# A graph network on one core: squares of the second edge layer summed on VectorE, scatters in chunks of their own

## The chip, the cores and the metric

The kernel runs on one core of one Trainium2 chip. The metric is device time in microseconds of one execution, from which the median of several runs is taken; smaller is better. The engines are PE (TensorE: matrix products, with its weight loads shown apart as PEld), DVE (VectorE), ACT (ScalarE), POOL (GpSimd) and SP (SyncE, here only a queue of DMA issues).

## The reference

Four graph layers follow one another on 12,500 nodes of 32 features and 400,000 edges that are sorted by their destination, each with a residual and a layer norm behind it. The change lies in the second of them and reaches back into the first. Cut to that:

```python
x = _layernorm(x + agg0)                      # layer 0: agg0[dst] += (x * out_norm)[src], times in_norm
row, col = edge_index                         # src, dst
h = concatenate([x[row], edge_attr_32], 1)    # 400000 x 64
h = lrelu(bn(h, g1, b1) @ w1 + c1)            # first edge layer,  64 -> 64
h = lrelu(bn(h, g2, b2) @ w2 + c2)            # second edge layer, 64 -> 64, slope 0.1
h = bn(h, g3, b3) @ w3 + c3                   # needs mean and mean square of h over the edges
agg = segment_sum(h, col)                     # 12500 x 64
h2 = concatenate([x, agg], 1)                 # node layers: three more products with bn before each
...
x = _layernorm(x + out)
```

The third layer (attention) wants the edges sorted by their source. For it the kernel builds a bucket sort: each edge's pair (src, dst) is written to a computed place of a table in HBM.

## The kernel before

**Tiling.** 400,000 edges are 625 groups of 640 edges: 128 partitions by T = 5. A loop turn takes SLOTS = 5 groups (ITERS = 125 turns), and each of its five slots has its own buffers. Every stage is a block in which each engine runs its own hand-written program; semaphores tie them together, and all engines meet between stages.

**Sums over destinations.** Nodes lie in 98 blocks of 128. A group touches one block, or a few. `one_hot` (line 107) compares the group's destination keys with a ramp 0..127, less the block's start, on DVE; it takes two tensors, `keys` and `ramp`, and a column of `starts` as scalar. PE multiplies the one-hot by the group's rows into PSUM bank 7 (line 162), and DVE adds the bank to the accumulator `acc` (line 138). There are 722 such visits for 625 groups: 97 times the group crosses into a further block, and then PE waits for a second one-hot. Layer 0 (`stage_convolve`) and the second edge layer (`stage_edges_second`) use these helpers. In layer 0, POOL gathers the rows by indirect DMA, five of 128 rows for each group (line 547).

**The second edge layer**, for each group: SP loads the activations `a1` of the first edge layer from HBM and the group's `pair` (lines 823, 826). PE multiplies them by the folded weights into bank 0 or 1 (line 898). DVE adds the bias row (`lift2`, line 874), makes the one-hot (line 107), and takes max(lift, 0.1 lift) into `rows` (line 879). ACT squares the rows (line 844), and PE sums the squares over the edges with products of 64 by 1 (line 906). Then comes the visit (lines 162 and 138). PE and DVE run one group ahead with the first half and one behind with the second (`in_turn`).

**The scatters.** Beside this, POOL issues for every group five indirect DMAs that write 128 pairs each to the bucket table (line 921), 3,125 in all. Their places come from `places`, which the first edge layer computed as floats; ACT turns a group's five columns into integers (`place`, line 838), in program order between two squares, and waits there until the slot's former scatters have landed:

```python
for j in range(SLOTS):
    square(i, j)
    act.wait_ge(s["moved"][j], 16 * T * (i + 1))
    place(i + 1, j)
```

**The node layers** (`stage_nodes`) follow: sums, transposes slab by slab, three products over 25 chunks of 500 nodes, and a layer norm. POOL has no program in this stage. After it `stage_source_keys` reads the bucket table.

## Time and profile before

| what | value |
|---|---|
| time, median of 3 runs | 29849.66 us (29847.4 to 29855.73) |
| profiled execution, its own time (first to last instruction) | 29897.7 us |
| PE busy over the whole | 24784.2 us (83%) |
| DVE busy | 17947.6 us (60%) |
| POOL busy | 16752.9 us (56%) |
| ACT busy | 4472.9 us (15%) |
| layer 0, first to last gather | 903.9 to 4884.5 us |
| second edge layer, first to last scatter | 9108.2 to 13208.2 us |
| node layers | 13220 to 13725 us |

All times inside the profile count from the span's start. "Busy" sums the instructions of an engine; "idle before" is what the engine stood still ahead of a group of instructions, with what ended it. On POOL, "issue" is the time between one indirect DMA and the next in which it waited for nothing that the profile shows.

### The profile page before, as it was taken

How to read it: one execution, taken by the hardware profiler on the slowest of the kernel's cores; microseconds unless marked ns; L12 is line 12 of the kernel's file. 1: busy time of each engine (PE TensorE's matmuls, PEld its weight loads, DVE VectorE, ACT ScalarE, POOL GpSimd, SP SyncE). 2: the span in 40 equal slices, each digit the busy share in tenths (PEclk: the TensorE clock that was granted, in tenths of full speed). 3: DMA queues.
4: the chain of work that ended last, by engine and by line, in shares of the span. 5: the costliest groups of instructions: out<-in, count | busy, mean ns of one | idle time of the engine just before them, and what ended most of it. 6: DMA issues, size and time to landing. Idle time of an engine off the chain costs nothing. (4 is left out here: it accounts for less than half of the span.)

```text
span 29897.7 us, 608296 instructions
## 1 busy us (share of the span) xinstructions
PE 24784.2 (83%) x149627; PEld 16178.0 (54%) x149628; DVE 17947.6 (60%) x47075; ACT 4472.9 (15%) x12240; POOL 16752.9 (56%) x16857
## 2 busy tenths in 40 slices
PE   8777776666668999986999998665888898898988
PEld 6444443222227888863666776664444444444444
DVE  9311114666664333333666665887777777778777
ACT  4111111111110000001111111221111111111111
POOL 0677776777777777752777776453333333333332
PEclk9555555555555555555666555997999999999999
DMA  2111112222221111103333336553333333333332
GB/s 66 36 30 30 30 30 44 51 50 50 51 50 28 27 27 27 27 17 41 80 79 80 79 78 64 164 172 107 74 75 74 74 73 74 74 75 75 73 75 68
DMA packets 2615646, 1869.05 MB, mean 63 GB/s; under 512 B 1600555, under 2 KB 2081065, under 8 KB 2613814
## 3 DMA queue, kind: packets, MB, share of 16 engines
q1 hardware_dynamic: 1914438, 1424.41, 19.2%
q0 software_dynamic: 516000, 217.22, 7.1%
q10 hardware_dynamic: 184400, 220.54, 2.9%
q14 instruction: 776, 6.36, 0.1%
q8 instruction: 32, 0.52, 0.0%
HBM read 1621.01 MB, written 238.82 MB: 62 GB/s over the span
## 5 line engine op out<-in xcount | busy, mean ns | idle before, releaser
L2069 POOL DMA_INDIRECT rows_x<-x_table,index x3125 | 3044.3, 974 | 6251.2 <-DMA index<-in_src 5485.0
L1310 POOL DMA_INDIRECT rows<-x_table,index x3625 | 3446.2, 951 | 2029.3 <-issue 1255.0
L162 PE MATMUL banks<-rows,onehot 128*128 128x33 f32 (+1 forms) x14440 | 3416.9, 413 | 1065.9 <-issue 592.0
L547 POOL DMA_INDIRECT rows<-x_table,index x3125 | 3029.3, 969 | 1853.6 <-issue 928.2
L162 PEld LDWEIGHTS banks<-rows,onehot 128*128 128x128 f32 x14440 | 3186.1, 328 | 1374.0 <-issue 1364.7
L921 POOL DMA_INDIRECT bucket_pairs<-pair,place_int x3125 | 3148.4, 1007 | 1012.2 <-issue 952.5
L696 POOL DMA_INDIRECT rows<-x_table,index x3125 | 3143.5, 1006 | 1019.6 <-issue 952.0
L1929 PE MATMUL banks<-first,same_unit 128*128 128x384 f32 (+1 forms) x10000 | 3504.7, 476 | 0.0
L1220 DVE CUSTOM_DVE_ANT_0 junk<-banks,mask 128x320 f32<-128x320 f32 x5800 | 2551.6, 487 | 1560.6 <-PE banks L1255 1538.5
L1778 DVE TENSOR_TENSOR second<-banks,h 128x384 f32<-128x384 f32 (+1 forms) x5000 | 2276.1, 485 | 690.5 <-PE banks L1929 681.1
L1770 DVE TENSOR_TENSOR first<-banks,h 128x768 f32<-128x768 f32 x2500 | 2054.9, 822 | 836.7 <-issue 442.5
L138 DVE TENSOR_TENSOR acc<-acc,banks 128x33 f32 (+1 forms) x1444 | 298.4, 207 | 3388.3 <-PE banks L162 3388.3
L1929 PEld LDWEIGHTS banks<-first,same_unit 128*128 128x128 f32 x10000 | 1824.2, 203 | 895.5 <-issue 511.3
L1917 PE MATMUL banks<-u_turned,w_tensor 32*128 32x384 f32 (+1 forms) x10000 | 2096.2, 496 | 250.1 <-DVE first L1770 235.3
L1255 PE MATMUL banks<-x_turned,vectors_wide 32*128 32x320 f32 x11600 | 2163.4, 718 | 0.0
L107 DVE SCALAR_TENSOR_TENSOR onehot<-keys,starts,ramp 128x640 f32<-128x640 f32 x1444 | 1279.1, 886 | 1344.5 <-issue 1344.5
L790 PE MATMUL banks<-ident,rows 128*64 128x128 f32 x3125 | 777.7, 415 | 1276.2 <-DMA rows<-x_table,index 1276.2
L1244 PE MATMUL banks<-ident,rows 128*32 128x128 f32 x29000 | 1542.0, 388 | 316.3 <-DMA rows<-x_table,index 314.1
L1244 PEld LDWEIGHTS banks<-ident,rows 128*32 128x32 f32 x29000 | 1189.4, 156 | 904.3 <-issue 846.5
L1267 PEld LDWEIGHTS banks<-vectors_four,x_turned 32*128 32x128 f32 x7250 | 1405.3, 282 | 346.8 <-issue 346.8
L1917 PEld LDWEIGHTS banks<-u_turned,w_tensor 32*128 32x128 f32 x10000 | 779.1, 190 | 1413.6 <-DVE first L1770 790.6
L1427 PE MATMUL banks<-rows,onehot 128*128 128x132 f32 x7250 | 1099.8, 304 | 520.9 <-POOL rows L1363 517.0
(396 smaller groups left out, 38909.6 us busy)
## 6 DMA issues: line engine op xcount, KB each, us to landing
key_row<-key_rows SPq DMA_DIRECT2D x1450, 320.0 KB
h<-hidden_dram SPq DMA_DIRECT2D x10000, 40.0 KB
key_row<-dst_rows SPq DMA_DIRECT2D x625, 320.0 KB
rows<-x_table,index POOLq DMA_INDIRECT x9875
a_dram<-a ACTq DMA_DIRECT2D x625, 160.0 KB
a<-a_dram SPq DMA_DIRECT2D x625, 160.0 KB
rows_dram<-rows ACTq DMA_DIRECT2D x725, 90.0 KB
x_rows<-rows_dram SPq DMA_DIRECT2D x725, 90.0 KB
```

What stands on the lines that cost most here:

```text
L162: mm = nc.tensor.matmul(m["ps"][7][:, 0:width], m["onehot"][j % 3][:, t * P:(t + 1) * P], rows[:, t, :], start=t == 0, stop=t == T - 1)
L547: nc.gpsimd.indirect_dma_start(out=m["rows"][j][:, t * W:t * W + F], out_offset=None, in_=m["x_table"], in_offset=bass.IndirectOffsetOnAxi ...
L696: nc.gpsimd.indirect_dma_start(out=m["rows"][j][:, t * C2:t * C2 + F], out_offset=None, in_=m["x_table"], in_offset=bass.IndirectOffsetOnA ...
L921: nc.gpsimd.indirect_dma_start(out=m["bucket_pairs"], out_offset=bass.IndirectOffsetOnAxis(ap=m["place_int"][j][:, t:t + 1], axis=0), in_= ...
L1220: nc.vector.tensor_tensor_reduce(m["junk"][j % 3][:, HALF * u:HALF * (u + 1)], bank(j, u), m["mask"][j % 3][:, HALF * half:HALF * (half + 1)],
L1244: mm = nc.tensor.matmul(m["ps"][6 + t // 4][F * h:F * (h + 1), t % 4 * P:(t % 4 + 1) * P], m["rows"][j][:, t * XA:t * XA + F], m["ident"][ ...
L1255: nc.tensor.matmul(bank(j, half * HEADS + h), m["vectors_wide"][rows, h * P:(h + 1) * P], m["x_turned"][j][rows, half * HALF:(half + 1) * ...
L1310: nc.gpsimd.indirect_dma_start(out=m["rows"][j][:, t * XA:t * XA + F], out_offset=None, in_=m["x_table"], in_offset=bass.IndirectOffsetOnA ...
L1778: nc.vector.tensor_tensor(m["second"][2 * (q % 2) + k][:, columns(half)], m["ps"][6 + k][:, 0:HALVES[half][1]], m["h2"][j][:, columns(half ...
L1917: mm = nc.tensor.matmul(m["ps"][4 + k][:, 0:HALVES[half][1]], m["w_tensor"][rows, chunk * P:(chunk + 1) * P], m["u_turned"][j % 3][rows, c ...
L1929: nc.tensor.matmul(m["ps"][6 + k][:, 0:width], m["same_unit"][:, :], m["first"][q][:, k * width:(k + 1) * width], start=True, stop=True).t ...
L2069: nc.gpsimd.indirect_dma_start(out=m["rows_x"][j][:, t * F:(t + 1) * F], out_offset=None, in_=m["x_table"], in_offset=bass.IndirectOffsetO ...
```

## The change

- The sum of squares leaves PE: ACT writes the squares into PSUM bank 5, and DVE adds them to `square_acc`, 128 by 320, for each group. After the loop PE sums that once, with five products.
- The bias becomes a 65th row of the weights, against a row of ones in `a1`. DVE's pass of line 874 goes. ACT makes 0.1 times the product (`lift2`), and DVE takes the maximum of the product in PSUM and `lift2`.
- The ramp is copied into PSUM bank 4, and `one_hot` reads it there, in layer 0 too.
- The places are written as integers in the first edge layer, and ACT's conversion goes. Pairs and places are loaded by SP in chunks of 25 columns, five chunks in flight, with no tie to the groups; ACT's queue issues the loads of `a1`.
- The scatters split: 22 turns of 125 (2,750) in the second edge layer, and 3 turns (375) in the node layers.
- PE's next product into a bank now waits for `a2_made`, the maximum, where it waited for `lifted`.

```diff
+RAMP_BANK = 4
 def one_hot(nc, m, g, j, at):
     return nc.vector.scalar_tensor_tensor(cut(m["onehot"][j % 3][:, :], t=T), rep(m["keys"][:, bass.ds(T * g, T)], 2, P),
-                                          m["starts"][:, bass.ds(at, 1)], rep(m["ramp"][:, :], 1, T),
+                                          m["starts"][:, bass.ds(at, 1)], rep(m["ps"][RAMP_BANK][:, 0:P], 1, T),
                                           ALU.subtract, ALU.is_equal)
...
             link(nc.vector.memset(m["acc"][:, 0:NB * W], 0.0))
+            link(nc.vector.tensor_copy(m["ps"][RAMP_BANK][:, 0:P], m["ramp"][:, :]))
...
-    nc.vector.tensor_reduce(m["places"][:, bass.ds(g * T, T)], cut(m["picked"][:, :], t=T), AX.X, ALU.add).then_inc(s["placed"], 1)
+    with nc.allow_low_precision(reason="one term of each sum is a whole number below 2 ** 24, the others are zero"):
+        nc.vector.tensor_reduce(m["places"][:, bass.ds(g * T, T)], cut(m["picked"][:, :], t=T), AX.X, ALU.add).then_inc(s["placed"], 1)
...
+SCATTER_FIRST = 22
+SCATTER_LAST = ITERS // SLOTS - SCATTER_FIRST
+def scatter_loads_sp(sp, m, s, first, turns):
+
+    width = SLOTS * T
+
+    def load(i, k):
+        at = ((first + i) * SLOTS + k) * width
+        sp.dma_start(m["pair"][k][:, :], m["pairs"][:, bass.ds(2 * at, 2 * width)]).then_inc(s["pair_in"][k], 16)
+        sp.dma_start(m["place_int"][k][:, :], m["places"][:, bass.ds(at, width)]).then_inc(s["pair_in"][k], 16)
+    for k in range(SLOTS):
+        load(0, k)
+    with sp.Fori(1, turns) as i:
+        for k in range(SLOTS):
+            sp.wait_ge(s["moved"][k], 16 * width * i)
+            load(i, k)
+
+
+def scatter_pool(nc, pool, m, s, turns):
+
+    width = SLOTS * T
+    with pool.Fori(0, turns) as i:
+        for k in range(SLOTS):
+            pool.wait_ge(s["pair_in"][k], 32 * (i + 1))
+            pool.sem_inc(s["going"], 1)
+            for c in range(width):
+                nc.gpsimd.indirect_dma_start(
+                    out=m["bucket_pairs"], out_offset=bass.IndirectOffsetOnAxis(ap=m["place_int"][k][:, c:c + 1], axis=0),
+                    in_=m["pair"][k][:, 2 * c:2 * c + 2], in_offset=None,
+                ).then_inc(s["moved"][k], 16)
+    for k in range(SLOTS):
+        pool.wait_ge(s["moved"][k], 16 * width * turns)
+
+
...
             sp.dma_start(m["sb_m1_c2"][:, :], m["m1_c2"].broadcast_to([P, H])).then_inc(s["weights"], 16)
-
-            def load(i, j, again):
-                g = SLOTS * i + j
-                sp.wait_ge(s["products"][j], ONE + i)
-                sp.dma_start(m["a1"][j][:, :], m["a1_dram"][bass.ds(g, 1)].rearrange("g h e -> (g h) e")).then_inc(s["a1_in"][j], 16)
-                if again:
-                    sp.wait_ge(s["moved"][j], 16 * T * i)
-                sp.dma_start(m["pair"][j][:, :], m["pairs"][:, bass.ds(g * 2 * T, 2 * T)]).then_inc(s["pair_in"][j], 16)
-            for j in range(SLOTS):
-                load(0, j, False)
-            with sp.Fori(1, ITERS) as i:
-                for j in range(SLOTS):
-                    load(i, j, True)
+            scatter_loads_sp(sp, m, s, 0, SCATTER_FIRST)
...
-            def place(i, j):
-                nc.scalar.copy(m["place_int"][j][:, :], m["places"][:, bass.ds((SLOTS * i + j) * T, T)]).then_inc(s["placed"][j], 1)
-
-            def square(i, j):
+            def load(i, j):
+                act.dma_start(m["a1"][j][0:H, :], m["a1_dram"][bass.ds(SLOTS * i + j, 1)].rearrange("g h e -> (g h) e")
+                              ).then_inc(s["a1_in"][j], 16)
+
+            def lift(i, j):
                 g = SLOTS * i + j
+                act.wait_ge(s["products"][j], ONE + i + 1)
+                act.wait_ge(s["a2_made"], ONE + g)
+                nc.scalar.activation(m["lift2"][:, :], m["ps"][j % 2][:, 0:T * H], ACT.Copy, scale=SLOPE).then_inc(s["lifted"], 1)
+
+            def square(i, j, again):
+                g = SLOTS * i + j
+                if again:
+                    load(i + 1, j)
                 act.wait_ge(s["a2_made"], ONE + g + 1)
                 act.wait_ge(s["squares_used"], ONE + g)
-                nc.scalar.square(cut(m["squares"][:, :], t=T), cut(m["rows"][j][:, 0:T * W], t=T)[:, :, 0:H]).then_inc(s["squared"], 1)
+                nc.scalar.square(cut(m["ps"][5][:, 0:T * H], t=T), cut(m["rows"][j][:, 0:T * W], t=T)[:, :, 0:H]).then_inc(s["squared"], 1)
+            act.wait_ge(s["unit_rows"], ONE + 1)
             for j in range(SLOTS):
-                place(0, j)
+                load(0, j)
+            lift(0, 0)
             with act.Fori(0, ITERS - 1) as i:
                 for j in range(SLOTS):
-                    square(i, j)
-
-                    act.wait_ge(s["moved"][j], 16 * T * (i + 1))
-                    place(i + 1, j)
+                    lift(i + (j + 1) // SLOTS, (j + 1) % SLOTS)
+                    square(i, j, True)
             for j in range(SLOTS):
-                square(ITERS - 1, j)
+                if j < SLOTS - 1:
+                    lift(ITERS - 1, j + 1)
+                square(ITERS - 1, j, False)
...
             link(nc.vector.memset(m["acc"][:, 0:NB * W], 0.0))
+            link(nc.vector.tensor_copy(m["ps"][RAMP_BANK][:, 0:P], m["ramp"][:, :]))
+            link(nc.vector.memset(m["square_acc"][:, :], 0.0))
+            for j in range(SLOTS):
+                link(nc.vector.memset(m["a1"][j][H:H + 1, :], 1.0))
+            nc.vector.nop().then_inc(s["unit_rows"], 1)
...
-            link(nc.vector.tensor_tensor(m["bias_row"][:, :], m["sb_m1_c2"][:, :], m["ps"][0][:, 0:H], ALU.add))
...
             def ahead(i, j):
                 g = SLOTS * i + j
-                dve.wait_ge(s["products"][j], ONE + i + 1)
-                dve.wait_ge(s["a2_made"], ONE + g)
-                nc.vector.tensor_tensor(cut(m["lift2"][:, :], t=T), cut(m["ps"][j % 2][:, 0:T * H], t=T),
-                                        rep(m["bias_row"][:, :], 1, T), ALU.add).then_inc(s["lifted"], 1)
                 hot_dve(nc, dve, m, s, g, j)
                 dve.wait_ge(s["lifted"], ONE + g + 1)
-                lift = cut(m["lift2"][:, :], t=T)
-                nc.vector.scalar_tensor_tensor(cut(m["rows"][j][:, 0:T * W], t=T)[:, :, 0:H], lift, SLOPE, lift,
-                                               ALU.mult, ALU.max).then_inc(s["a2_made"], 1)
-            in_turn(dve, ahead, lambda i, j: visits_dve(nc, dve, m, s, SLOTS * i + j, j, m["acc"], W))
+                nc.vector.tensor_tensor(cut(m["rows"][j][:, 0:T * W], t=T)[:, :, 0:H], cut(m["ps"][j % 2][:, 0:T * H], t=T),
+                                        cut(m["lift2"][:, :], t=T), ALU.max).then_inc(s["a2_made"], 1)
+
+            def behind(i, j):
+                g = SLOTS * i + j
+                visits_dve(nc, dve, m, s, g, j, m["acc"], W)
+                dve.wait_ge(s["squared"], ONE + g + 1)
+                dve.wait_ge(s["squares_used"], ONE + g)
+                nc.vector.tensor_tensor(m["square_acc"][:, :], m["square_acc"][:, :], m["ps"][5][:, 0:T * H], ALU.add
+                                        ).then_inc(s["squares_used"], 1)
+            in_turn(dve, ahead, behind)
             sums_done(nc, dve, m, s)
-            dve.wait_ge(s["squares_used"], ONE + GROUPS)
+            dve.wait_ge(s["square_totals"], ONE + 1)
             nc.vector.tensor_copy(m["square_sum"][0:H, :], m["ps"][2][0:H, 0:1])
...
-            nc.tensor.matmul(m["ps"][2][0:H, 0:1], m["zeros"][:, 0:H], m["zero_row"][:, 0:1], start=True, stop=False, skip_group_check=True)
...
             def ahead(i, j):
                 pe.wait_ge(s["a1_in"][j], 16 * (i + 1))
-                pe.wait_ge(s["lifted"], ONE + (SLOTS * i + max(j - 1, 0)))
+                pe.wait_ge(s["a2_made"], ONE + (SLOTS * i + max(j - 1, 0)))
                 for t in range(T):
-                    mm = nc.tensor.matmul(m["ps"][j % 2][:, t * H:(t + 1) * H], m["a1"][j][:, t * P:(t + 1) * P],
-                                          m["w"][0:H, 0:H], start=True, stop=True)
+                    mm = nc.tensor.matmul(m["ps"][j % 2][:, t * H:(t + 1) * H], m["a1"][j][0:W, t * P:(t + 1) * P],
+                                          m["w"][0:W, 0:H], start=True, stop=True)
                 mm.then_inc(s["products"][j], 1)
             def behind(i, j):
                 g = SLOTS * i + j
-                pe.wait_ge(s["squared"], ONE + g + 1)
-                for t in range(T):
-                    mm = nc.tensor.matmul(m["ps"][2][0:H, 0:1], m["squares"][:, t * H:(t + 1) * H], m["ones"][:, 0:1],
-                                          start=False, stop=False, skip_group_check=True)
-                mm.then_inc(s["squares_used"], 1)
                 pe.wait_ge(s["a2_made"], ONE + g + 1)
                 visits_pe(nc, pe, m, s, g, j, cut(m["rows"][j][:, 0:T * W], t=T), W)
             in_turn(pe, ahead, behind)
+            pe.wait_ge(s["squares_used"], ONE + GROUPS)
+            for t in range(T):
+                mm = nc.tensor.matmul(m["ps"][2][0:H, 0:1], m["square_acc"][:, t * H:(t + 1) * H], m["ones"][:, 0:1],
+                                      start=t == 0, stop=t == T - 1)
+            mm.then_inc(s["square_totals"], 1)
         @block.gpsimd
         def _(pool):
-            with pool.Fori(0, ITERS) as i:
-                for j in range(SLOTS):
-                    pool.wait_ge(s["placed"][j], ONE + i + 1)
-                    pool.wait_ge(s["pair_in"][j], 16 * (i + 1))
-                    pool.sem_inc(s["going"], 1)
-                    for t in range(T):
-                        nc.gpsimd.indirect_dma_start(
-                            out=m["bucket_pairs"], out_offset=bass.IndirectOffsetOnAxis(ap=m["place_int"][j][:, t:t + 1], axis=0),
-                            in_=m["pair"][j][:, 2 * t:2 * t + 2], in_offset=None,
-                        ).then_inc(s["moved"][j], 16)
-            for j in range(SLOTS):
-                pool.wait_ge(s["moved"][j], 16 * T * ITERS)
+            scatter_pool(nc, pool, m, s, SCATTER_FIRST)
...
             sp.wait_ge(s["cleared"], ONE + 1)
             sp.dma_start(m["c3_row"][H:H + 1, :], m["m1_c3"]).then_inc(s["weights"], 16)
+            scatter_loads_sp(sp, m, s, SCATTER_FIRST, SCATTER_LAST)
+
+        @block.gpsimd
+        def _(pool):
+            scatter_pool(nc, pool, m, s, SCATTER_LAST)
...
         sb("acc", NB * (H + 1), into=whole)
+        sb("places", COLS, I32, into=whole)
+        for name, cols in (("pair", 2 * SLOTS * T), ("place_int", SLOTS * T)):
+            m[name] = [whole.enter_context(nc.sbuf_tensor(f"{name}{k}", [P, cols], I32)) for k in range(SLOTS)]
```

## Rows read from the trace of the kernel before

**Rows 1.** Window of the second edge layer: us, busy of PE, PEld, DVE, ACT, POOL, granted clock.
```profile
9109.00:13209.00 4100.00, 3867.08 (x19722) 3682.89 (x19721) 1360.06 (x2695) 394.62 (x1245) 3147.46 (x3125) 0.50 0.13 26
```

**Rows 2.** Groups of the second edge layer: busy us, mean ns, idle before.
```profile
L921 POOL DMA_INDIRECT bucket_pairs<-pair,place_int x3125 | 3148.4, 1007 | 1012.2 <-issue 952.5 <-ACT place_int L838 59.7
L162 PE MATMUL banks<-rows,onehot 128*128 128x65 f32 x7220 | 1727.8, 423 | 171.9 <-DVE onehot L107 171.9
L898 PE MATMUL banks<-w,a 64*128 64x64 f32 x6250 | 1494.9, 423 | 0.2 <-DVEq L868 0.2
L906 PE MATMUL banks<-ones,squares 128*64 128x1 f32 x6250 | 765.4, 247 | 59.7 <-ACT squares L844 59.7
L107 DVE SCALAR_TENSOR_TENSOR onehot<-keys,starts,ramp 128x640 f32<-128x640 f32 x722 | 639.9, 886 | 407.5 <-issue 407.5
L874 DVE TENSOR_TENSOR lift<-banks,bias_row 128x320 f32<-128x320 f32 x625 | 307.4, 492 | 1224.2 <-PE banks L898 1224.1
L879 DVE SCALAR_TENSOR_TENSOR rows<-lift 128x320 f32<-128x320 f32 x625 | 302.7, 484 | 0.0
L844 ACT ACTIVATE squares<-rows 128x320 f32<-128x320 f32 x625 | 293.5, 470 | 61.0 <-DVE rows L879 32.5 <-issue 25.2
L138 DVE TENSOR_TENSOR acc<-acc,banks 128x65 f32 x722 | 161.2, 223 | 1107.4 <-PE banks L162 1107.4
```

**Rows 3.** Line 921, all scatters: ns min/median/max, first and last start.
```profile
L921 POOL DMA_INDIRECT bucket_pairs<-pair,place_int x3125: 954/958/1609, 9108.2 to 13208.2; - x196
```

**Rows 4.** Timeline of one turn: start, duration, engine, line, and what released it.
```profile
11002.12 2.39 PE L898 MATMUL banks<-w,a 64*128 64x64 f32 x10
...
11004.45 1.23 PE L906 MATMUL banks<-ones,squares 128*64 128x1 f32 x10
11004.55 0.49 DVE L874 TENSOR_TENSOR lift<-banks,bias_row 128x320 f32<-128x320 f32 x1 [1.98 <-PE banks L898]
11004.58 0.96 POOL L921 DMA_INDIRECT bucket_pairs<-pair,place_int  x1 [0.30 <-issue]
...
11005.60 2.39 PE L162 MATMUL banks<-rows,onehot 128*128 128x65 f32 x10
11005.70 0.89 DVE L107 SCALAR_TENSOR_TENSOR onehot<-keys,starts,ramp 128x640 f32<-128x640 f32 x1 [0.65 <-issue]
11005.85 1.57 POOL L921 DMA_INDIRECT bucket_pairs<-pair,place_int  x1 [0.30 <-issue]
...
11007.92 2.39 PE L898 MATMUL banks<-w,a 64*128 64x64 f32 x10
```

**Rows 5.** First and last of the 196 long scatters in 9500 to 11500.
```profile
9508.28 1.28 POOL L921 DMA_INDIRECT bucket_pairs<-pair,place_int  x1 [0.30 <-issue]
...
11495.42 1.20 POOL L921 DMA_INDIRECT bucket_pairs<-pair,place_int  x1 [0.30 <-issue]
```

**Rows 6.** Line 547, the gathers of the first stage of sums: ns min/median/max, idle.
```profile
L547 POOL DMA_INDIRECT rows<-x_table,index x3125: 940/944/1605, 903.9 to 4884.5; - x196
...
  issue: 928.2, 3045
```

**Rows 7.** Timeline at the start and the end of the second edge layer.
```profile
9100.49 0.59 SPq L826 DMA_DIRECT2D pair<-in_pairs  x1
...
9109.54 4.52 PE L898 MATMUL banks<-w,a 64*128 64x64 f32 x20 [0.23 <-DVEq L868]
...
13219.94 0.50 SPq L944 DMA_DIRECT2D sb_m_w<-in_m_w  x1
```

**Rows 8.** Timeline of the node layers: last load, last VectorE work, next stage.
```profile
13229.75 0.28 SPq L946 DMA_DIRECT2D c_row<-in_m_c  x1
...
13713.36 3.43 DVE L91 TENSOR_TENSOR tmp<-x 128x3136 f32<-128x3136 f32 x1
...
13726.56 0.40 SPq L315 DMA_DIRECT2D block_dram<-block_int  x1
```

**Rows 9.** Group of the node layers' bend, over 13209.5 to 13726.
```profile
L1030 DVE SCALAR_TENSOR_TENSOR h<-node_lift 96x500 f32 x50 | 33.7, 675 | 128.2 <-ACT node_lift L965 128.2
```

15 lines of the change are left out of this document (7 added, 8 removed).

## The prediction

> **What bounds the kernel now.** I read the page first: over the whole, PE is the busiest engine, but that is a mean over eight stages. The change touches three of them (layer 0, the second edge layer, the node layers), so each is read by itself. In the second edge layer the window shows PE 3867 of 4100 us busy and POOL 3147, at a granted clock of 0.50, TensorE's lower level of 1.2 GHz [rows 1]. Busy time misleads here, because issue time does not count. The groups show it: the 3,125 scatters are busy 3148.4 us and have 952.5 us of issue ahead of them [rows 2], together 4100.9 us. That is the whole way from the first scatter at 9108.2 to the end of the last at about 13209.1 [rows 3]. POOL never waits for another engine after its start. It is the bound, at 4100.9 / 3,125 = 1.312 us a scatter.
>
> PE is close behind. One group without a second visit takes 11007.92 - 11002.12 = 5.80 us on PE: 2.32 for line 898, 1.16 for line 906, 2.32 for line 162 [rows 4]. The 97 further visits cost 171.9 / 97 = 1.77 us of waiting for the one-hot and 2.32 us of product each. 625 x 5.80 + 97 x 4.09 + 59.7 of waiting for squares [rows 2] = 3625 + 397 + 60 = 4082 us, against 4098 from 9109.5 to 13207.8. So the wait for squares is all the slack PE has: ACT's conversion of places, in program order between the squares, holds PE to POOL's pace. Taking 725 us off PE alone would bring at most that little; the scatters must go too.
>
> **Scatters that take longer.** The scatter has a median of 958 ns and a mean of 1007, with a maximum of 1609 [rows 2, 3]: 3,125 x 0.049 = 153 us are lost to long ones. In the turn shown, the long scatter starts at 11005.85, inside the one-hot of 11005.70 to 11006.59, and ends 0.83 us after that one-hot; the scatter at 11004.58 runs beside line 874 and takes its 0.96 us [rows 4]. Between 9500 and 11500, 196 of 1,524 scatters are over 1.01 us [rows 5], and 194 of them started while a one-hot was running (two beside line 879 alone, whose input lies twice in SBUF); of 256 that started beside line 138 or 874, with one operand in PSUM, none was long. The gathers of layer 0 show the same: median 944 ns, maximum 1605 [rows 6]. My reading: a DVE instruction with two tensors in SBUF keeps POOL from reading its indices.
>
> The Trainium skill, "SBUF — State Buffer", section "Who interferes with whom", says as much: a DVE instruction with two SBUF inputs contends with a GpSimd instruction that reads SBUF, one with at most one does not. By that rule all long scatters vanish with the ramp in PSUM, and the sum comes out as below.
>
> **Part by part. Scatters in the second edge layer.** 2,750 remain. The pitch without long ones is 0.958 + 952.5 / 3,124 = 1.263 us, so 2,750 x 1.263 = 3473 us. The kept DVE work has one operand in PSUM in every instruction of the loop (one-hot, maximum, addition to `acc`, addition of squares). The unknown is whether the one-hot, which still has `keys` and the scalar column in SBUF, lets POOL through. Bounds: fully, as beside lines 138 and 874, 3473; not at all, 2,750 x 1.312 = 3609, 136 more. I take the first, since those rows are the nearest in kind. Below it, the least duration of 954 ns [rows 3] would give another 11. Waiting every 25 scatters in place of every 5 I cost at nothing: the issue time before the scatters is the same 0.30 whether a group begins or not. The first scatter no longer waits for ACT's conversion: SP's queue reached its first pair at 9100.49 [rows 7]; with its place load behind it (0.59 to issue) and some 2 us to land it starts between 9102 and 9108; I take 9104. End: 9104 + 3473 = 12577, against 13209: **-632 us**.
>
> **PE must keep ahead of that.** Line 906 goes (1.16 us a group); line 898 has 65 rows for 64, at no cost, as line 162 with 128 rows has the same mean of 423 ns [rows 2]. 625 x 4.64 + 397 = 3297 us. It starts later than 9109.5 [rows 7] by DVE's new preparation (a copy, six fills); seven times the 0.89 of the 640 elements of line 107 is the most, nothing the least; I take 4. End: 9113.5 + 3297 = 12411, 166 us ahead of POOL, or 0.27 us a group. This slack covers the new waits. For the slot that wraps (j = 0), PE needs the maximum of the group just multiplied: 2.43 us from line 898's start to its reader's [rows 4], 0.49 for the lift on ACT (470 ns for a square of this size), 0.49 for the maximum (492 for line 874), some 0.3 of handing over: 3.7, while PE has 2.32 + 2.32 = 4.64 us of other work. DVE does, in each group, 722 / 625 x (0.886 + 0.564 issue + 0.223) + 2 x 0.49 = 2.9 us; ACT two passes of 0.47 to 0.49 and one issue of at most 0.59, about 1.6. Both lie inside 4.64. If the cover were gone, each us a group would cost 625. The `a1` loads, moved from SP's queue to ACT's, are issued more than three groups (14 us) before their use; SP's queue, which now waits for landed scatters, has only scatter loads behind that wait.
>
> The ramp in PSUM may slow the one-hot. Line 874, with a PSUM operand, takes 492 ns, line 879, with none, 484 [rows 2]: 8 ns for 320 elements, so some 10 to 16 ns, in work that DVE does inside PE's 4.64 us.
>
> The Trainium skill, "VectorE: DVE Perf Modes", section "The TRN2 errata", gives 120 fixed cycles for a PSUM source and 58 for an SBUF source, an estimate of 65 ns more a one-hot. These rows do not show it (8 ns); by the page the further visits would cost PE 97 x 0.065 = 6 us, inside the slack as well.
>
> **Layer 0.** From the first gather to the last, 4884.5 - 903.9 = 3980.6 us for 3,124 pitches; at 0.944 + 928.2 / 3,045 = 1.249 us [rows 6] they take 3901. **-79 us** if the one-hot lets POOL through, 0 if not. POOL is the bound: the issue rows and its durations fill the stage.
>
> **Node layers.** The 375 scatters start behind SP's last weight load at 13229.75 (times of before) [rows 8]: two issues of 0.59 and some 2 us give 13233. 375 x 1.263 = 474, to 13707. The bend of line 1030 has both tensors in SBUF, 50 times 0.675 us [rows 9]. A start falls inside one with a chance of 0.675 / 1.263 and loses 0.34: 9 us, 13716. Then the layer norm's passes of 3.43 us, such as 13713.36 [rows 8], can hold back what is left: three of them have two SBUF tensors, 10 us at most, with the landing 13728, while before the next stage starts at 13726.56. Between 0 and 15; I take **+2**. DVE's own delay by POOL is within this: the one-hot's maximum in such company stayed under 1 us.
>
> **Sum.** -632 - 79 + 2 = -709. The profiled execution has a span of 29897.7, 48 us (0.16%) above the median of the runs; it would come to 29189, and the median to 29849.7 - 709 = **29141 us**, 2.4% faster.
>
> **Rivals.**
> 1. *The one-hot still blocks POOL*, by `keys` or by the scalar column. For it: I have no row with one SBUF tensor, a scalar column and a PSUM tensor. Against: lines 138 and 874 block nothing. Price: 136 + 79 = 215, so 29356.
> 2. *The node layers do not hide the scatters*: the many small chained DVE steps and POOL hold each other up, or the scatters start late. For it: POOL ends within 10 us of the stage. All 375 uncovered would add 474; I price a quarter, 120: 29261.
> 3. *The PE loop becomes the bound*, because bank, ACT and DVE form a chain in each group: 2.43 + 0.49 + 0.49 + 0.3 + 2.32 = 6.03 us. Then the loop takes 625 x 6.03 + 397 = 4166, ends at 13280, 71 later than before, and with layer 0 the time is 29844: no change. It shows from 4.90 us a group on. Against: the order of `in_turn` puts a product of the other group under the chain.
> 4. *Slower*: the same chain also takes in the square on ACT and its addition on DVE, because each waits for the other through the single `lift2` and bank 5: 6.03 + 0.47 + 0.49 + 0.2 = 7.2 us a group. 625 x 7.2 + 397 = 4897, end 14011, +802 - 79 + 2: 30575. It decides from 6.04 us a group. Against it speaks that the sum of squares comes behind the visit in DVE's order, a whole PE product after its input.
>
> **How the numbers follow.** Forecast 0.75, rival 1 0.10, rival 2 0.07, rival 3 0.05 (of which 0.03 lands within 0.2%), rival 4 0.03. The forecast's own range is 29113 (least durations, earliest start) to 29170 (preparation at its most, 15 us in the node layers, some long scatters left). With rivals 1 and 2 the range is 29112 to 29360. A difference under 0.2% (60 us) is about what a measurement of this kernel cannot tell from none. Faster 0.94, same 0.03, slower 0.03.
>
> **What would show it.** Scatters of line 921 with a maximum near 970 ns in the second edge layer, and a stage 632 us shorter; gathers of layer 0 near 0.944 each and the stage 79 us shorter; PE's group at 4.64 us, with idle time it did not have; node layers of about 505 us with 375 scatters in them. I am wrong if scatters over 1.1 us remain beside the one-hots, if PE's groups take 4.9 us or more, or if the stage after the node layers starts more than 15 us late.

## The result and the profile after

The changed kernel takes 29103.83 us (median of 4 runs, 29053.54 to 29111.04) beside 29848.53 us for the kernel before (4 runs): ratio 0.9746, 95% interval 0.9734 to 0.9758, 745 us faster. The forecast was 29141 us with a range from 29112: the direction and nearly the whole size are as forecast, but the time lies 37 us below the forecast and 8 us below the range. The profiled execution of the changed kernel took 29098.85 us (a span of 29096.7 from first to last instruction), that of the kernel before has a span of 29897.7.

Groups of the second edge layer in the changed kernel (9020 to 12517 us), beside [rows 2]:
```profile
L840 POOL DMA_INDIRECT bucket_pairs<-pair,place_int x2750 | 2641.9, 961 | 892.3 <-issue 837.2 <-DMA place_int<-places 55.0
L165 PE MATMUL banks<-rows,onehot 128*128 128x65 f32 x7220 | 1695.4, 418 | 172.6 <-DVE onehot L110 172.1 <-DVE acc L141 0.5
...
L945 PE MATMUL banks<-w,a 65*128 65x64 f32 x6250 | 1460.3, 421 | 0.7 <-DVEq L913 0.7
...
L110 DVE SCALAR_TENSOR_TENSOR onehot<-keys,starts,banks 128x640 f32<-128x640 f32 x722 | 635.4, 880 | 478.3 <-issue 478.3
L919 DVE TENSOR_TENSOR rows<-banks,lift 128x320 f32<-128x320 f32 x625 | 305.5, 489 | 22.2 <-ACT lift L874 14.7
L927 DVE TENSOR_TENSOR square_acc<-square_acc,banks 128x320 f32<-128x320 f32 x625 | 304.7, 488 | 153.3 <-issue 146.4
L882 ACT ACTIVATE banks<-rows 128x320 f32<-128x320 f32 x625 | 275.9, 442 | 193.4 <-issue 190.8 <-DVE square_acc L927 2.6
L874 ACT ACTIVATE lift<-banks 128x320 f32<-128x320 f32 x625 | 273.6, 438 | 2330.9 <-PE banks L945 2330.9
L141 DVE TENSOR_TENSOR acc<-acc,banks 128x65 f32 x722 | 160.7, 223 | 1043.1 <-PE banks L165 1043.1
```
The mean scatter has gone from 1007 to 961 ns, and the group of squares has left TensorE. POOL still never waits for an engine once it runs. ACT's lift (line 874, 0.1 times the product) and square take 0.44 us each in the mean, and the maximum of line 919 waits 14.7 us in all for the lifts.

The windows of 1000 us in the middle of the stage, of the kernel before and of the changed one (us, then busy us and count of PE, PEld, DVE, ACT, POOL, granted clock, DMA share, GB/s):
```profile
10000.00:11000.00 1000.00, 942.69 (x4811) 897.76 (x4812) 332.96 (x659) 96.13 (x304) 767.64 (x763) 0.50 0.13 27
```
```profile
10000.00:11000.00 1000.00, 943.32 (x4385) 937.44 (x4385) 448.42 (x878) 178.87 (x408) 759.40 (x791) 0.50 0.16 35
```
POOL issues 791 scatters where it issued 763. The granted clock is 0.50 in both, the lower level of 1.2 GHz, so the clock gives nothing here.

One turn of the changed kernel, beside [rows 4]:
```profile
11000.72 2.34 PE L945 MATMUL banks<-w,a 65*128 65x64 f32 x10
...
11002.75 0.88 DVE L110 SCALAR_TENSOR_TENSOR onehot<-keys,starts,banks 128x640 f32<-128x640 f32 x1 [0.65 <-issue]
11002.85 2.34 PE L165 MATMUL banks<-rows,onehot 128*128 128x65 f32 x10
11002.92 0.96 POOL L840 DMA_INDIRECT bucket_pairs<-pair,place_int  x1 [0.30 <-issue]
...
11004.99 1.27 PE L945 MATMUL banks<-w,a 65*128 65x64 f32 x5
```
The scatter at 11002.92 starts inside the one-hot and takes 0.96 us, where its like in [rows 4] took 1.57. PE's group is 11004.99 - 11000.72 = 4.27 us; the prediction had 4.64.

All scatters of the changed kernel, those beside the node layers included, and the gathers of layer 0 (ns min/median/max, first and last start), beside [rows 3, 6]:
```profile
L840 POOL DMA_INDIRECT bucket_pairs<-pair,place_int x3125: 955/962/4077, 9026.6 to 13007.7; - x196
```
```profile
L551 POOL DMA_INDIRECT rows<-x_table,index x3125: 941/947/1092, 902.8 to 4810.8; - x196
```

Of the 2,750 scatters in the second edge layer none is over 1.01 us (before: 407 of 3,125). The 13 that are lie beside the node layers: 12 start inside the bend (line 1030 before, 1071 here), which reads two SBUF tensors, and the one of 4077 ns is shown below.

Start and end of the second edge layer and of the node layers, beside [rows 7, 8]:
```profile
9020.40 0.50 SPq L858 DMA_DIRECT2D sb_m_w<-in_m_w  x1
...
9026.57 1.00 POOL L840 DMA_INDIRECT bucket_pairs<-pair,place_int  x1 [55.04 <-DMA place_int<-places]
...
12110.55 1.23 PE L956 MATMUL banks<-ones,square_acc 128*64 128x1 f32 x10 [1.22 <-DVE square_acc L927]
...
12504.71 0.96 POOL L840 DMA_INDIRECT bucket_pairs<-pair,place_int  x1 [0.30 <-issue]
12517.71 0.51 SPq L980 DMA_DIRECT2D sb_m_w<-in_m_w  x1
...
12530.52 0.96 POOL L840 DMA_INDIRECT bucket_pairs<-pair,place_int  x1 [24.85 <-DMA place_int<-places]
...
13007.54 3.42 DVE L90 TENSOR_TENSOR x<-x,mean 128x3136 f32<-128x3136 f32 x1
13007.72 4.08 POOL L840 DMA_INDIRECT bucket_pairs<-pair,place_int  x1 [0.31 <-issue]
...
13024.27 0.40 SPq L318 DMA_DIRECT2D block_dram<-block_int  x1
```
From SP's first DMA of one stage to that of the next, the second edge layer takes 12517.71 - 9020.40 = 3497.3 us (before 4122.4), the node layers 13024.27 - 12517.71 = 506.6 us, exactly as before (13726.56 - 13219.94 [rows 7, 8]), with 375 scatters in them. The last of these meets a layer-norm step with two SBUF tensors: it takes 4.08 us and ends 0.84 us after that step, the same tail as that of the long scatters before; there was room for it.

Where the time came from (us, from the first profiles of the two kernels; the attention gather and the tensor product are counted from their first gather to their last, and the attention sum is what lies between them):

| | before | after | forecast | measured |
|---|---|---|---|---|
| layer 0, first to last gather | 3980.6 | 3908.0 | -79 | -72.6 |
| second edge layer | 4122.4 | 3497.3 | -632 | -625.1 |
| node layers | 506.6 | 506.6 | +2 | 0.0 |
| start of the source keys' stage | 13726.6 | 13024.3 | -709 | -702.3 |
| attention gather | 4763.2 | 4748.0 | 0 | -15 |
| attention sum | 2113.5 | 2070.3 | 0 | -43.2 |
| tensor product | 9001.4 | 8962.6 | 0 | -39 |

Not all of these repeat. Two more profiles of the kernel before and one more of the changed program (before_again, before_b and pad_pe below) have 4744 to 4763 us in the attention gather against 4748 to 4752, so no difference; 8978 to 9014 in the tensor product against 8960 to 8963; 2109 to 2115 in the attention sum against 2068 to 2070; and in layer 0 3977 to 3981 against 3900 to 3908.

### The profile page after: what moved, and what is told of

It is laid out like the page before. It is cut to its first block and busy times, and to the rows that moved or that the text cites. A ratio compares the mean times of both kernels' runs of the same rounds, so it can differ in the third digit from the quotient of the medians.

```text
span 29096.7 us, 592714 instructions
## 1 busy us (share of the span) xinstructions
PE 23725.4 (82%) x143386; PEld 15329.1 (53%) x143387; DVE 17957.4 (62%) x47083; ACT 4626.8 (16%) x12240; POOL 16532.3 (57%) x16857
## 5 line engine op out<-in xcount | busy, mean ns | idle before, releaser
L840 POOL DMA_INDIRECT bucket_pairs<-pair,place_int x3125 | 3009.3, 963 | 1031.0 <-issue 951.1
L110 DVE SCALAR_TENSOR_TENSOR onehot<-keys,starts,banks 128x640 f32<-128x640 f32 x1444 | 1270.8, 880 | 1398.0 <-issue 1398.0
```

Source lines behind the costliest of these rows:

```text
L840: nc.gpsimd.indirect_dma_start(out=m["bucket_pairs"], out_offset=bass.IndirectOffsetOnAxis(ap=m["place_int"][k][:, c:c + 1], axis=0), in_= ...
```

## The experiments

Two conditions of the machine were met, and the reader needs them for the numbers. The comparison above and two more sessions (one with before_again, the ramp kernels and no_split, one with before_b, compute_only and pad_pe) found the kernel before at 29,849 to 29,900 us; I call this the undisturbed condition. Three others found it at 35,788, 36,242 and 35,802 us, every run of them alike; the first of these was on the chip that in a later session gave 29,856. I call that the other condition. Whole times are compared only within a session, as ratios or differences to the kernel before of that session; durations of stages are compared across sessions of one condition.

**The kernel before once more** (before_again, before_b; no edit).

> The kernel before, unchanged, for its stages. From the start of the stage behind the node layers to the end it took 16171 us in the first profile, and the changed kernel took 16072 there with the same code. Theory A (executions differ by chance in these stages): this profile shows 16110 to 16150 there, and the time is within 0.1% of before. Theory B (the change shortens the later stages too): it shows 16171 again, within 10 us.

> The kernel before, for its trace. If the chip is one of the slower kind (some 36,000 us): theory, that GpSimd's unbroken stream of scatters holds back the semaphores of TensorE, expects its second edge layer near 5,100 us (35,788 us less the other stages of the changed kernel's trace there), thus 1,500 us less than the changed kernel's 6,625, with groups that wait on other engines less than the changed kernel's 56 us a group. Rival: that chip's loads are slow for both; then TensorE waits for its load of a1 (landing well over the 13 us after issue seen in the changed kernel on both kinds of chip). If the chip is of the first kind: 29,850 to 29,900 us, the second edge layer 4,122 us, the attention sum 2,113 us.

Measured: 29881.27 us, ratio 1.0 (0.9991 to 1.001), and 29868.42 us, ratio 1.0004 (0.9994 to 1.0014). So two sets of ten and more runs of one kernel agree within 0.1%; with four runs the interval is some 0.17% either way. The second edge layer took 4122.0 and 4122.9 us, the attention sum 2114.5 and 2108.7, within 6 us of the first profile. From the start of the source keys' stage to the end it is 16145 and 16158 us where the first profile has 16171. The 16145 lies in the interval of theory A: a part of what the first pair of profiles shows in these stages is chance. The changed program has 16072 and 16073 (pad_pe) there, so 72 to 99 us of difference are left, which repeats alone do not explain.

**The ramp alone** (ramp_only: before, with this) and **the ramp taken back** (ramp_back: after, without it).
```
-  ... rep(m["ramp"][:, :], 1, T), ...
+  ... rep(m["ps"][RAMP_BANK][:, 0:P], 1, T), ...
```


> The kernel before with the ramp in PSUM alone. Port theory (a one-hot with two SBUF tensors keeps POOL from starting a DMA): long scatters and gathers vanish, layer 0 is 73 us shorter. In the second edge layer POOL needs only 3,125 x 1.265 = 3953 us, PE needs 625 x 5.80 + 397 = 4022, so PE becomes the bound and the stage is 60 to 78 us shorter: 133 to 151 us in all. Rival (the ramp matters in layer 0 alone, since in the second layer the in-place maximum of line 879, twice from SBUF, blocks as well): 73 us in all.

> The changed kernel with the ramp read from SBUF again. Port theory: layer 0 is 73 us longer; in the second edge layer 722 one-hots at up to 0.21 us each stretch the scatters by 110 to 154 us, and POOL is the bound, so 183 to 227 us slower. Rival (the second layer's gain came from the other DVE edits): 73 us slower, with a mean scatter of 961 ns left.

Measured: 29739.12 us, ratio 0.9941 (0.9924 to 0.9957), 161 us faster than before (median 29900.49), with layer 0 at 3903.3 and the second edge layer at 4045.7 us. Taken back: 29344.65 us, 0.9812 (0.9796 to 0.9828); layer 0 3988.5, second edge layer 3645.3 us, that is 80.5 and 148 us more than in the changed kernel. The gathers of layer 0 with it taken back, then the scatters of the ramp alone:
```profile
L551 POOL DMA_INDIRECT rows<-x_table,index x3125: 940/945/1608, 903.4 to 4892.0; - x196
```
```profile
L926 POOL DMA_INDIRECT bucket_pairs<-pair,place_int x3125: 953/959/1285, 9033.6 to 13035.1; - x196
```
The maximum is back at 1608 in the one. In the other it falls to 1285: what is left are 182 scatters over 1.01 us, and all of them start inside line 884, which is this kernel's line 879 with its two SBUF operands; of the 424 that start inside a one-hot none is long. A one-hot with `keys` and the scalar column in SBUF but the ramp in the accumulator banks (PSUM) lets POOL through. Rival 1 did not come. The traces also say which starts are hit: in the kernel before, of the scatters that start in the first 0.1 us of a one-hot 0 of 167 are long, and of those that start between 0.1 and 0.7 us after its start all 395. Beside line 884 of ramp_only the edge lies earlier: all 35 that start 0.04 to 0.1 us into it are long. The Trainium skill, "SBUF — State Buffer", section "Who interferes with whom", has this rule of two SBUF inputs, and these runs agree with it.

**No scatters beside the node layers** (no_split).
```
-SCATTER_FIRST = 22
+SCATTER_FIRST = 25
```


> The changed kernel with all 3,125 scatters in the second edge layer and none beside the node layers. Theory (POOL is the bound of the second layer and the node layers hide theirs for nothing): 375 x 1.265 = 474 us slower, the node layers unchanged at 506.6 us. Rival (the 375 cost the node layers something, or PE bounds the second layer in part): clearly less, 430 us or under.

Measured: 29575.79 us, 0.9887 (0.9871 to 0.9904). The second edge layer took 3962.7 us, 465 more than after: 375 x 1.265 = 474 but for the landing. The node layers took 507.3 us without a scatter and 506.6 with 375. They hide all of them, so rival 2 did not come. This part is 465 us of the stage; of the whole time it is 420 us, by the differences to the kernel before in each session (325 us faster here, 745 for the changed kernel). The two medians themselves lie 472 us apart, but the kernel before also stood 52 us higher among the runs of no_split.

**The change without its scatter part** (compute_only: places converted on ACT, a pair tile a group, none beside the node layers; squares, bias row and ramp as changed).
```
 after's stage, with
+                    act.wait_ge(s["moved"][j], 16 * T * (i + 1))
+                    place(i + 1, j)
-            scatter_pool(nc, pool, m, s, SCATTER_FIRST)
+            with pool.Fori(0, ITERS) as i: ...   # as before
```


> The changed kernel with the scatters as in the kernel before (groups of five behind a conversion of the places on ScalarE, one pair tile a group, a1 from SyncE's queue, none beside the node layers); the squares, the bias row and the ramp stay changed. Chip of the first kind: GpSimd bounds the second edge layer at 625 x 6.35 to 6.47 = 3,970 to 4,045 us, the kernel 150 to 230 us faster than before plus 43 us of the attention sum: some 190 to 270 us faster. Chip of the slower kind: if the unbroken stream of scatters is what loses there, this kernel is faster than before (ratio 0.98 to 1.00) while the changed kernel stands at 1.05; if it is the squares or the bias edit, it stands near 1.05 too. The attention sum is near 2,070 to 2,080 us if the squares and bias edit is what shortens it, near 2,115 us if it is the scatter part.

Measured: 29575.25 us, 0.9903 (0.9886 to 0.9919), 281 us faster than before. Its scatters:
```profile
L941 POOL DMA_INDIRECT bucket_pairs<-pair,place_int x3125: 954/958/992, 9024.5 to 12968.1; - x196
```
3,125 at 1.262 us, no long one, stage 3970.9 us. In no_split, with chunks of 25, the way from the first scatter to the last is the same 3943.6 us: the size of the chunk costs nothing in POOL's pace. The 8 us between the two stages (3962.7 in no_split) lie ahead of the first scatter, which starts 15.4 and 6.0 us after SP's first DMA of the stage. So of the change's 625 us in this stage, about 150 are the long scatters, 465 the scatters that moved out, and some 8 the start. The squares and the bias edit have no share of their own: they keep TensorE out of the way of the rest. In ramp_only, which has neither, TensorE's products run from 9041.5 to 13064.0, 4022 us as the prediction counts them for its old loop, and end 28 us after the last scatter. There TensorE holds the stage, and only 77 of the 150 us come out.

**The changed kernel with empty instructions on TensorE** (pad_pe).

> The changed kernel with 190 empty instructions at the end of TensorE's program of the second edge layer, about as many as the change took out of it. Theory, that the attention sum and the tensor product run faster in the changed kernel because TensorE's later loops lie elsewhere in its program: the attention sum goes back from 2,070 to about 2,113 us and the tensor product's gathers by some 25 us, so 40 to 70 us slower than the changed kernel. Rival: the place in TensorE's program is nothing, and the cause lies elsewhere (the moment at which the clock and the loops meet, or the other engines' programs): attention sum 2,070 to 2,080 us. The 190 instructions themselves cost a few us at most.

The 190 empty instructions left none in the trace, so this was the changed kernel once more, and tells nothing on its theory: 29096.76 us, 0.9741 (0.9725 to 0.9758), 760 us faster than the kernel before of its session; layer 0 3899.7, second edge layer 3489.7, attention sum 2067.6 us. The result repeats.

**The product over 64 rows** (rows64, run in two sessions; the bias row is left out of the computation), and **the scatter part alone** (scatter_only, likewise; the squares on TensorE and the bias on DVE as before). Both ran in the other condition of the machine only, where the last part of the stage, after its last scatter, shows TensorE's loop by itself.
```
-  m["a1"][j][0:W, t * P:(t + 1) * P], m["w"][0:W, 0:H]
+  m["a1"][j][0:H, t * P:(t + 1) * P], m["w"][0:H, 0:H]
```


> The changed kernel with the product of the second edge layer over 64 rows, which leaves the bias row out of the computation. The prediction took TensorE's group at 4.64 us, from rows of a loop that goes to and fro between products of 64 rows and of 128; measured was 4.27 us with 65 rows. Theory: the change between a product of 64 rows and one of 128 costs time at each passage (starts 0.35 instead of 0.21 us apart), and the 65th row does away with it: the group is near 4.6 us here (625 x 4.6 = 2,900 to 2,950 us of the loop), and the time of the kernel is unchanged, since the scatters still bound the stage (2,750 x 1.265 = 3,479 us). Rival: the gaps of before were waits for the squares or for the additions of the bias, now gone; then the group stays at 4.27 us.

> The kernel before with the scatter part of the change alone (places kept as whole numbers, chunks of 25 columns, 22 turns in the second edge layer and 3 beside the node layers, a1 loaded from ScalarE's queue); the squares stay on TensorE, the bias stays an addition on VectorE, and the ramp stays in SBUF. Theory of the prediction: what bounds the second edge layer is then TensorE's loop at its old pitch, 625 x 5.80 + 397 = 4,022 us, so the stage shrinks from 4,122 to some 4,020 to 4,060 us and the kernel gains 60 to 100 us. Rival: the placement of the scatters alone is worth most of the gain (2,750 x 1.33 with long first scatters = 3,660 us, kernel 460 us faster); then TensorE's old loop was never close behind. On the stages whose code is unchanged: if they are faster because of what the scatters' code does to the program (it is the longest new piece), the attention sum is near 2,070 us; if it is the squares' or the bias's edit, near 2,113 us.

The windows of 16000 to 17000 us, no scatter in them: the changed kernel, rows64, scatter_only.
```profile
16000.00:17000.00 1000.00, 943.31 (x4385) 937.43 (x4385) 448.25 (x877) 178.49 (x406) 0.00 (x0) 0.50 0.11 33
```
```profile
16000.00:17000.00 1000.00, 946.72 (x4068) 896.70 (x4067) 421.83 (x813) 165.49 (x377) 0.00 (x0) 0.50 0.11 31
```
```profile
16000.00:17000.00 1000.00, 957.54 (x4896) 914.25 (x4897) 337.00 (x669) 72.89 (x156) 0.00 (x0) 0.50 0.09 26
```
With 4385 products in 1000 us the changed kernel goes at exactly the pace of its undisturbed run. rows64 does 4068: its group without a second visit takes 4.65 us against 4.27. The starts of the products stand 0.213 us apart inside a run of one kind in both. At the passage from line 945 to 165 and back they stand 0.347 us apart with 64 rows and 0.213 with 65, and with 64 rows the next start after it comes 0.269 us later instead of 0.213. So a passage between 64 and 128 rows costs 0.134 + 0.056 = 0.19 us, two of them a group are the 0.38 us between 4.65 and 4.27, and the 65th row does away with them. Both runs of rows64 and the kernel before (from line 162 to 898 and from 898 to 906) have the same 0.347. The Trainium skill, "TensorEngine Tiling (Array Packing)", section "Key Properties", says that a change of tiling mode drains TensorE. The page doesn't say that a plain product over 64 rows between two over 128 is such a change; these rows behave as if it were, and put 0.19 us on it at the lower clock.

scatter_only has groups of 5.80 us, as in [rows 4], and a mean of 6.45 with the second visits: 625 x 6.45 = 4031 us is an estimate of what TensorE would have needed with the scatters gone and its squares kept. It agrees with the 4022 us of ramp_only in the undisturbed condition, and with the prediction's reading that TensorE was close behind POOL; the whole of scatter_only was not seen in that condition.

**A third place for scatters** (tables_host, three sessions): the attention tables' stage ahead of that of the source keys, with 3 chunks beside it and 107 in the second edge layer.
```
+            scatter_loads_sp(sp, m, s, SCATTER_FIRST + NODE_CHUNKS, TABLE_CHUNKS)
+            scatter_pool(nc, pool, m, s, TABLE_CHUNKS)
```


> The changed kernel with the stage of the attention tables ahead of that of the source keys, and a third place for scatters beside it: 107 chunks of 25 in the second edge layer, 15 beside the node layers, 3 beside the attention tables. Theory, that GpSimd's pitch bounds the second edge layer and the others hide scatters: second edge layer 75 x 1.265 = 95 us shorter (3,402 us), the tables' stage 89 us before and some 100 to 105 here (75 x 1.265 = 95 us and their landing), so 80 to 85 us faster than the changed kernel. Rival: the scatters beside the tables hold back its own DMAs or the addition of two tables, so that the stage grows by 30 us or more and the gain is under 60 us.

> The changed kernel with the stage of the attention tables ahead of that of the source keys, and a third place for scatters beside it: 107 chunks of 25 in the second edge layer, 15 beside the node layers, 3 beside the attention tables. Theory, that GpSimd's pitch bounds the second edge layer and the others hide scatters: second edge layer 95 us shorter than the changed kernel's 3,490 to 3,497 us (3,395 to 3,402), the tables' stage some 10 to 15 us longer, so 80 to 85 us faster than the changed kernel: 29,015 to 29,025 us, ratio 0.9715 to 0.972 where the changed kernel had 0.9741 to 0.9746. In the slow sessions the second edge layer was 93 to 101 us shorter. Rival: the scatters beside the tables hold back its own DMAs or the addition of two tables, so that the stage grows by 30 us or more and the gain is under 60 us (ratio 0.9725 or more).

All three met the other condition: 37558.96 against the changed kernel's 37587.54 us, 37999.55 against 38000.2, 37629.95 against 37616.97 for pad_pe2, below. The second edge layer was 93 to 125 us shorter each time; in the first session the way from the node layers' last scatter to the attention gather was 85 us longer (698 against 613). No gain there; whether it gains the 80 us in the undisturbed condition was not measured.

**The changed kernel in the other condition** (after_again, after_third; no edit).

> The changed kernel unchanged, beside the others of this group of runs. Expected within 0.2% of the earlier comparison's ratio to the kernel before (0.9746), second edge layer 3,497 us from SyncE's first DMA of the stage to the node layers' first, node layers 506.6 us. If the two runs of the kernel before (29,848 and 29,900 us) differ because the chips differ, the changed kernel should also stand some 50 us higher here than 29,104 us; if instead about 43 us of the gain in the attention sum and 30 in the tensor product belong to the changed kernel, its attention sum is again near 2,070 us against 2,113 in the kernel before.

Measured: 37587.54 us, ratio 1.0503 (1.0485 to 1.052), and 38000.2 us, 1.0488 (1.0467 to 1.051). The expectation of 0.9746 was missed: here the change is a loss of 5%. scatter_only stands at 1.0763 and 1.0734, rows64 at 1.0562 and 1.0548; as scatter_only has none of the other edits, the loss goes with the scatter part. The changed kernel's second edge layer takes 6625 us. Here are two windows beside the scatters, then a stretch of the timeline without POOL's rows:
```profile
11820.00:12820.00 1000.00, 78.02 (x341) 74.27 (x342) 36.25 (x70) 14.93 (x34) 751.79 (x715) 0.50 0.04 5
12820.00:13820.00 1000.00, 84.72 (x370) 80.41 (x370) 38.00 (x72) 14.05 (x32) 755.52 (x713) 0.50 0.04 5
```
```profile
11024.40 2.40 PE L165 MATMUL banks<-rows,onehot 128*128 128x65 f32 x10 [49.16 <-issue]
...
11026.59 2.34 PE L945 MATMUL banks<-w,a 65*128 65x64 f32 x10
...
11079.51 0.22 DVE L141 TENSOR_TENSOR acc<-acc,banks 128x65 f32 x1 [26.46 <-DMA rows<-x_table,index]
...
11079.79 2.40 PE L165 MATMUL banks<-rows,onehot 128*128 128x65 f32 x10 [50.85 <-issue]
...
11081.98 2.34 PE L945 MATMUL banks<-w,a 65*128 65x64 f32 x10
...
11107.50 0.44 ACT L874 ACTIVATE lift<-banks 128x320 f32<-128x320 f32 x1 [54.23 <-DMA index<-in_src]
...
11107.97 0.49 DVE L919 TENSOR_TENSOR rows<-banks,lift 128x320 f32<-128x320 f32 x1 [26.02 <-issue]
...
11135.79 0.23 DVE L141 TENSOR_TENSOR acc<-acc,banks 128x65 f32 x1 [27.33 <-DMA rows<-x_table,index]
```
While POOL scatters (715 in 1000 us, not much slower than 791), the other engines do about a twelfth of their work; when it stops they are back at full pace. The stage is a sum, POOL's 3830 us and then 2790 us of TensorE's, where it should be a maximum. The waits named are DMAs of other stages, so the releaser is not known to the profile. What the timeline shows, with each wait put to the product that it waits for (by its place in the loop and by the slot's semaphore): the product of line 165 that ends at 11026.80 is added at 11079.51, 53 us later, and the product of line 945 that ends at 11028.93 is lifted at 11107.50, 79 us later. Over all 65 groups that TensorE does beside the scatters the medians are 53.4 and 78.6 us; in the undisturbed run they are 0.2 and 0.1. What waits for ACT or DVE starts at once (11107.50 to 11107.97, 11079.51 to the next product). The readers start at points 28 us apart (11079.5, 11107.5, 11135.8). The loads are not late: by the times of their packets, a load of a1 is through 2.2 us after its issue in both runs (median). So the completion of TensorE's work is what reaches the others late.

It is not bound to this stage or to scatters. In layer 0, beside the gathers, the product that ends at 2504.00 is added at 2515.79, after a run of nine gathers:
```profile
2501.66 2.34 PE L165 MATMUL banks<-rows,onehot 128*128 128x33 f32 x10
...
2515.79 0.19 DVE L141 TENSOR_TENSOR acc<-acc,banks 128x33 f32 x1 [13.12 <-remote]
```
39% of layer 0's additions come over 1 us late there and none in the undisturbed run. Layer 0 takes 5113 us instead of 3908, the attention gather 7108 instead of 4748, and the node layers with their 375 scatters 932 instead of 507. The kernel before has such stages too, and is slow here as well. On the same chip it lost 5,932 us (35787.95 against 29856.38) and the changed program 8,491 (37587.54 against 29096.76), of which 3,135 are in the second edge layer and 425 in the node layers. If the other stages lose the same in both, the kernel before lost some 1,000 us in its second edge layer, which is an estimate: no trace of it was had there. A reason may be that its scatters hang on ACT's conversions, so that late completions hold POOL up and it lets them through; that is argued and not shown. What puts the machine into this condition stays open.

**Where the 43 us of the attention sum come from** (pad_pe2, pad_da2: the changed kernel, with increments of a semaphore that nobody waits for, at the end of the programs of the second edge layer, where these engines have 390 us to spare).
```
pad_pe2:  +            for _ in range(193):
          +                pe.sem_inc(s["going"], 1)
pad_da2:  + 40 times dve.sem_inc(...) at VectorE's end, 40 times act.sem_inc(...) at ScalarE's
```


> The changed kernel with 193 increments of a semaphore that nobody waits for at the end of TensorE's program of the second edge layer, about as many instructions as the change took out of it. TensorE is done with that stage some 390 us before GpSimd, so they cost nothing there. Theory, the place of TensorE's later loops in its program is what makes the attention sum faster: it goes back to about 2,113 us, and the kernel is 40 to 70 us slower than the changed kernel. Rival: it is not, attention sum 2,068 to 2,072 us.

> The changed kernel with 40 such increments at the end of VectorE's and of ScalarE's programs of the second edge layer. Theory, the place of VectorE's or ScalarE's later loops decides: the attention sum moves by 10 us or more from 2,070 us (to 2,113 us if the place of before happens to be met in kind). Rival: it stays at 2,068 to 2,072 us, and the cause is none of these places. 40 increments cost 2 us at most, hidden behind GpSimd's scatters.

Both met the other condition, which the attention sum hardly feels (2080.4 and 2078.4 us in after_again and after_third). Measured: pad_pe2 37616.97 us, attention sum 2070.8; pad_da2 37832.91 us, attention sum 2125.0. One group of VectorE's instructions in the attention sum (busy, mean | idle before), in the first profile of the kernel before, then in the changed kernel, pad_pe2 and pad_da2:
```profile
L1352 DVE TENSOR_SCALAR hot_turned<-key_row,part 128x640 bf16<-128x640 f32 x725 | 398.2, 549 | 47.9 <-issue 47.7
```
```profile
L1393 DVE TENSOR_SCALAR hot_turned<-key_row,part 128x640 bf16<-128x640 f32 x725 | 398.1, 549 | 30.1 <-issue 29.9
```
```profile
L1395 DVE TENSOR_SCALAR hot_turned<-key_row,part 128x640 bf16<-128x640 f32 x708 | 388.9, 549 | 29.4 <-issue 29.4
```
```profile
L1397 DVE TENSOR_SCALAR hot_turned<-key_row,part 128x640 bf16<-128x640 f32 x663 | 364.2, 549 | 42.4 <-issue 42.4
```
The instruction itself takes 549 ns in all four. The issue time before it is 66 ns in the kernel before, 41 in the changed one and with TensorE's program lengthened, and 64 again with VectorE's and ScalarE's lengthened. By the stage tables, every kernel with the squares and bias edit has the attention sum at 2068 to 2089 us and every one without it at 2109 to 2122 us, pad_da2 alone excepted. So it is no fixed gain of the edit: 40 idle instructions more in each of these two engines' earlier programs take its 43 us away again, and the kernel is 216 us slower than pad_pe2 (37832.91 against 37616.97), 133 us of it in the tensor product, which differs by up to 39 us between other kernels of that session. Shown, by one profile of pad_da2, is that the length of VectorE's or ScalarE's earlier program can change the pace of later loops by as much as the change did. That this is also what happened between the kernel before and the changed one is likely but not shown; which of the two engines, and by what, is open. The issue rows speak for VectorE: 725 times 25 ns are 18 of the 43 us.

The granted clock is a rival. The attention sum and then the tensor product in the kernel before and in the changed one (columns as above):
```profile
18690.00:20797.00 2107.00, 1295.63 (x11300) 1195.20 (x11300) 1749.95 (x5289) 504.39 (x1636) 940.61 (x725) 0.86 0.52 150
20797.00:29898.00 9101.00, 8145.22 (x47080) 4414.65 (x47080) 7198.04 (x17176) 1377.50 (x3753) 3044.27 (x3125) 0.94 0.31 74
```
```profile
17970.00:20034.00 2064.00, 1261.93 (x11326) 1165.27 (x11318) 1745.67 (x5299) 505.05 (x1638) 922.51 (x725) 0.88 0.52 153
20034.00:29096.00 9062.00, 8103.16 (x47080) 4405.14 (x47080) 7191.85 (x17176) 1377.00 (x3753) 3041.87 (x3125) 0.95 0.30 75
```
In the attention sum the clock stands at its lower level (1.2 GHz) for 588 us in the kernel before and 579 in pad_da2, but for 505 in the changed kernel and 495 in pad_pe2. It does not explain the difference alone, for at the higher level (2.4 GHz) by itself VectorE starts 2.95 and 2.94 instructions a us in the first two and 3.02 in the others: the loop itself is faster, which is worth some 36 of the 43 us (an estimate: the 4,497 instructions that the kernel before starts at this level, at 3.02 in place of 2.95 a us). In the tensor product it is otherwise. There VectorE's pace at the higher level is 1.96 to 1.97 instructions a us with or without the edit, and the lower level lasts 919 to 1009 us in the four undisturbed profiles without the squares and bias edit and 828 to 887 in the five with it. So what is gained in the tensor product goes with the time at the lower clock; why that is shorter is open.

## Why the prediction was right, and where it failed

- **What bounds the stage**: right. POOL's 3,125 scatters at 1.312 us were it; after, 2,750 at 1.265 are, and TensorE ends 390 us earlier. The forecast end, 3473 us after the first start, was 3479.
- **The long scatters**: right in mechanism and size (expected 153 + 79; ramp_only shows 77 + 77, with TensorE's loop as the new bound of the second, ramp_back 148 + 80 with all else changed). The reading of [rows 4, 5], that lines with an operand in the accumulator banks let POOL through, carried over to a form that the trace did not hold. The prediction counts 256 scatters that started beside line 138 or 874; inside these instructions the trace has 186 starts from 9500 to 11500 (56 and 130). None is long, so the reading stands.
- **-632** was -625 and **-79** was -73 in the first profile, where each indirect DMA took 2 to 4 ns longer than in the other undisturbed runs (medians of 947 and 962 ns). The same program in pad_pe, with 944 and 958 ns, gives -633 and -81. **+2** was 0. That the sizes agree this closely is in part luck, the mechanism is not.
- **TensorE's group at 4.64 us** failed: 4.27. I counted the 65th row as free, with the mean of 423 ns as ground. It is better than free, since the passages between 64 and 128 rows cost 0.19 us each, and the 4.64 of [rows 4] has two of them in it. rows64 gives back 4.65. The error was covered by slack, and cost the forecast of the time nothing; in a kernel bound by TensorE it would have been 625 x 0.37 = 230 us.
- **The step that put the time below the range**: "The change touches three of them", with all other stages taken at their old times, a term of 0. At the start of the source keys' stage the sum was 7 us off. Behind it, unchanged code ran 99 us faster in the first profiles and 72 to 99 us among the repeats, most of it in the attention sum (some 43 us) and the tensor product (15 to 55 us). In the medians the gain came out 36 us larger than forecast. In the attention sum the loop itself was faster, and pad_da2 shows that the length of VectorE's or ScalarE's program ahead can do that; in the tensor product the clock stood at its lower level for less time, for a reason that is open. That the program's length was the cause between these two kernels is not shown. My range had a floor built of the changed stages' least prices alone (29 us below the forecast); a floor of 0.2% would have held it.
- **Rivals**: 1 is answered by the ramp runs, 2 by no_split, 3 and 4 by the group of 4.27 us, which lies under their 4.90 and 6.04: none came. None of them foresaw that the same change can lose 5% in another condition of the machine.

## What to carry to other kernels

When GpSimd issues small indirect DMAs without pause and bounds a stage, their count times the pitch (1.26 us here) is the price: move the issues beside stages where that engine is idle, and keep one of the two tensors that VectorE reads beside it in the accumulator banks. Look for the engine that is close behind; here it was TensorE, and without its squares moved out most of the gain would have stayed away. On TensorE, a row added to a 64-row product can be cheaper than none, if the products next to it use 128 rows. And when an edit lengthens or shortens an engine's program, allow later loops some 0.2% either way, and time such a kernel in more than one session before calling it better.
